# Sparse second feed-forward: a three-stage pair pipeline with six input slots, shared pairs first

## The reference, cut to what matters

```python
logits = x_flat @ gate_w.T                     # 16 experts in 4 groups
scores = sigmoid(logits)
# the best 2 of 4 groups, then the best 4 experts of these; weights renormed, times 2.5
inter = silu(g) * u                            # g, u: 256 -> 128, per expert
expert_out = inter @ down.T                    # 128 -> 256
y = sum over the 4 chosen experts of weight * expert_out
shared_out = silu(x @ shared_gate.T) * (x @ shared_up.T) @ shared_down.T
x = x + tanh(g_ffn[1]) * (y + shared_out)      # with x layer-normed ahead
```

## Time and profile before

| | us |
|---|---|
| median of 2 runs | 1687.89 (1682.67 to 1693.12) |
| the profiled execution's own time | 1683.4 |
| its span, from the first to the last instruction | 1681.6 |
| of it `moe`, from its first weight DMA to the end | 1084.1 to 1681.6 |

### The profile page before, as it was taken

The page is one execution under the profiler, slowest core; times in us unless marked ns, Lnnn a source line. Parts: engine busy times, 40 slices in busy tenths (PEclk is TensorE's granted clock), DMA queues, the critical chain, the costliest instruction groups (busy, mean ns, idle before and its releaser), DMA issues. The chain is left out here.

```text
span 1681.6 us, 27903 instructions
## 1 busy us (share of the span) xinstructions
PE 1214.9 (72%) x9252; PEld 1108.6 (66%) x9252; DVE 950.1 (56%) x2126; ACT 790.8 (47%) x2137; POOL 529.8 (32%) x590
## 2 busy tenths in 40 slices
PE   3675129995899999999999998667773545478772
PEld 2554128884788888888888887567663535367662
DVE  5886845551766666786677777556641212134664
ACT  4554125451566666666565655346442222245441
POOL 4342263642000010003530356163343342444432
PEclk8766559997999999999999999779886676789886
DMA  3354834545000000002420133276233333344785
GB/s 95 135 160 121 180 120 124 147 116 135 7 8 7 8 20 26 8 1 69 133 64 2 64 127 128 64 224 179 86 123 110 92 106 99 96 145 135 251 281 214
DMA packets 135394, 177.12 MB, mean 105 GB/s; under 512 B 17856, under 2 KB 116320, under 8 KB 135264
## 3 DMA queue, kind: packets, MB, share of 16 engines
q1 hardware_dynamic: 107888, 123.67, 25.3%
q0 software_dynamic: 17792, 43.14, 8.0%
q10 hardware_dynamic: 9584, 8.60, 1.6%
HBM read 107.28 MB, written 68.09 MB: 104 GB/s over the span
## 5 line engine op out<-in xcount | busy, mean ns | idle before, releaser
L1587 ACT ACTIVATE attend_s<-attend_s,attend_less 128x128 f32<-128x128 f32 x512 | 198.3, 391 | 107.8 <-DVE attend_less L1728 104.4
L2199 POOL DMA_INDIRECT answers<-moe_yb,moe_dst x160 | 156.4, 978 | 271.9 <-ACT moe_yb L2264 234.5
L2432 PE MATMUL moe_psX<-const_ident,moe_xg 128*128 128x128 f32 x384 | 71.4, 318 | 133.6 <-DMA moe_xg<-slots 126.7
L2313 DVE TENSOR_TENSOR moe_il<-moe_psI,moe_ih 128x256 fp32r<-128x256 f32 x96 | 40.4, 421 | 216.2 <-ACT moe_ih L2248 209.6
L1198 POOL DMA_INDIRECT slots<-router_row,router_idx x128 | 129.4, 1011 | 101.2 <-DMA router_row<-normed_rows 69.6
L1542 POOL TENSOR_TENSOR router_xn<-rest_acc,router_mv 128x512 f32<-128x512 f32 x12 | 12.5, 1045 | 447.5 <-DVE router_rs L1230 391.3
L2432 PEld LDWEIGHTS moe_psX<-const_ident,moe_xg 128*128 128x128 f32 x384 | 52.7, 163 | 137.1 <-DMA moe_xg<-slots 129.6
L81 PE MATMUL moe_psU<-moe_wh,moe_xl 128*128 (+1 forms) x384 | 131.5, 342 | 0.0
L82 PE MATMUL moe_psU<-moe_wl,moe_xh 128*128 (+1 forms) x384 | 120.2, 313 | 0.0
L83 PE MATMUL moe_psU<-moe_wh,moe_xh 128*128 (+1 forms) x384 | 119.5, 311 | 0.0
L81 PE MATMUL moe_psY<-moe_wh,moe_il 128*128 (+1 forms) x192 | 66.1, 344 | 66.8 <-DVE moe_il L2313 60.0
(11 more groups left out here) (367 smaller groups left out, 4209.4 us busy)
## 6 DMA issues: line engine op xcount, KB each, us to landing
moe_xg<-slots SPq DMA_DIRECT2D x160, 129.0 KB
router_row<-normed_rows SPq DMA_DIRECT2D x64, 256.0 KB
moe_big<-answers SPq DMA_DIRECT2D x16, 1024.0 KB
layer_raw<-in_wi_dram SPq DMA_DIRECT2D x8, 1024.0 KB, 5.0
layer_raw<-in_wo_dram SPq DMA_DIRECT2D x8, 1024.0 KB, 7.0
moe_raw<-in_gex_dram SPq DMA_DIRECT2D x17, 384.0 KB
slots<-moe_big SPq DMA_DIRECT2D x32, 129.0 KB
mix_xin<-in_x_dram SPq DMA_DIRECT2D x8, 512.0 KB, 3.8
```

Of the source, the lines that this page charges most:

```text
L1587: last = nc.scalar.activation(s[:, g, j, :], s[:, g, j, :], ACT.Exp, bias=less[:, g, j:j + 1], accum_out=sm[:, g, j:j + 1])
L2199: nc.gpsimd.indirect_dma_start(out=R.YT[q], out_offset=bass.IndirectOffsetOnAxis(ap=dst[:, j % NX, s:s + 1], axis=0), in_=yb[:, j % NY, s, ...
L2313: v.tensor_tensor(il[:], psI[:, 0:N], ih[:], ALU.subtract).then_inc(i_lo, 1)
L2432: last = nc.tensor.transpose(psX[j % 2][:, k * N + s * P:k * N + (s + 1) * P], xg[:, j % NX, s, k * P:(k + 1) * P], C["ident"][:])
```

## The change

Only `moe` and what feeds it change. The numbers of pairs and their order stay: all 16 shared pairs in front (`FIRST, LATE = 16, 0`).

1. Three stages in place of two. PE in turn j does `up(j)`, `turn(j+2)`, `turn_inner(j-1)`, `down(j-2)`; the loops run to 98 turns. `ih`, `il` get two buffers. ACT: `silu(j)`, `x_high(j+2)`, `i_high(j-1)`, `y_out(j-2)`.
2. NX 4 to 6, NY 3 to 5. Weight and target are no longer copied out: ACT and the indirect DMA read them from `xg` in place, the target as an integer. So a routed slot of `xg` is free only when the answers of its pair are written.
3. A shared pair is added by DVE straight from `psY`; POOL and ACT have no part in it.
4. The weights run at two experts a turn: the low half of the odd ones on POOL, between the sends of chunk 3.
5. The rows of the last chunk go through a ring of four (`row`, in the memory of `yt`), the sends begin at turn 22 instead of 27.
6. The padding comes from a DRAM tensor `fill`, written early in the kernel (four more DMAs there, 4.2 MB), DRAM to DRAM.
7. The answers come batch by batch (512 KB), three slots. The routing steps move ahead: 13, 15, 17, 20 in place of 18, 20, 22, 25.

```diff
-            sp.dma_start(rows_[:, :, 0:D], zero.unsqueeze(1).to_broadcast([P, E1, D])).then_inc(self.spare_in, 16)
-            sp.dma_start(rows_[:, :, D:WIDE], self.spare[:, q]).then_inc(self.spare_in, 16)
-        sp.wait_ge(self.spare_in, 64)
+            for kind, to in enumerate((self.fill[q], spare)):
+                rows_ = to.rearrange("(t p) n -> p t n", p=P)
+                sp.dma_start(rows_[:, :, 0:D], zero.unsqueeze(1).to_broadcast([P, E1, D])).then_inc(self.spare_in, 16)
+                sp.dma_start(rows_[:, :, D:WIDE], self.marks[:, q, kind]).then_inc(self.spare_in, 16)
+        sp.wait_ge(self.spare_in, 128)
...
-    NX, NY, NR = 4, 3, 2
-    CB = 2
+    NX, NY, NR, NT, NS = 6, 5, 2, 3, 4
...
-        exps_at, groups_at, experts_at, weights_at, placed_at = 17, 18, 20, 22, 25
+        exps_at, groups_at, experts_at, weights_at, placed_at = 11, 13, 15, 17, 20
...
+        def scattered(eng, r):
+            eng.wait_ge(y_free[r % NY], 32 * (r // NY + 1))
...
             def load(j):
                 b = j % NX
                 if j >= NX:
-                    sp.wait_ge(t_done, j - NX + 1)
+                    if is_shared(j - NX):
+                        sp.wait_ge(t_done, j - NX + 1)
+                    else:
+                        scattered(sp, NTH[j - NX])
...
-                if j - NX >= SHARED_PAIRS:
-                    sp.wait_ge(d_up, j - NX - SHARED_PAIRS + 1)
...
+            for j in range(NX, PAIRS_ALL):
+                i = j - NX
+                for k in (2 * i + NR, 2 * i + NR + 1):
+                    if k < EXPERTS:
+                        weights(k)
+                if j in (7, 9, 11):
+                    R.load_row(sp, LAST - 1, (j - 5) // 2, 0)
+                    R.load_row(sp, LAST - 1, (j - 5) // 2, 1)
+                if j in (8, 10, 12, 14):
+                    R.store_normed(sp, LAST, (j - 8) // 2)
...
+            for t in range(4):
+                R.send(pool, LAST - 1, t)
+                low(4 * t + 1)
+                low(4 * t + 3)
+            for j in ROUTED:
                 scatter(j)
+                i = j - sends_from
+                if i == 0:
+                    pool.wait_ge(R.idx_up, LAST + 1)
+                if 0 <= i < 2 * HALVES:
+                    if i % 2 == 0:
+                        mark(i // 2)
+                    send(i // 2, i % 2)
...
+            def add(j):
+                dve.wait_ge(y_done, j + 1)
+                a = rows(acc[:, 2 * NTH[j]:2 * NTH[j] + 2, :])
+                v.scalar_tensor_tensor(a, psY[j % 2][:], C["gate"][:, 3:4], a, ALU.mult, ALU.add).then_inc(added, 1)
...
+            for j in range(PAIRS_ALL + 2):
...
+                if j < PAIRS_ALL:
+                    up(j, bases[j])
...
                 if j + 2 < PAIRS_ALL:
                     turn(j + 2)
+                if 1 <= j <= PAIRS_ALL:
+                    turn_inner(j - 1)
+                if j >= 2:
+                    down(j - 2, bases.pop(j - 2))
```

More of the change, by code:

```diff
@@ L1087, in __init__ @@
         self.YT = [nc.dram_tensor(f"answers{q}", ((PART_B[q] * TOP + 2 * E1) * P, D), F32, kind="Internal").ap() for q in range(2)]
+        self.fill = [nc.dram_tensor(f"fill{q}", (E1 * P, WIDE), F32, kind="Internal").ap() for q in range(2)]
     def stage(self, m):
-        self.spare = m.sb("spare", [P, 2, E1, 2])
+        self.marks = m.sb("marks", [P, 2, 2, E1, 2])
         self.spare_up, self.spare_in = m.sem("spare_up"), m.sem("spare_in")
@@ L1094, in gpsimd @@
         nc = self.nc
-        nc.gpsimd.memset(self.spare[:], 0.0).then_inc(self.spare_up, 1)
+        nc.gpsimd.memset(self.marks[:], 0.0).then_inc(self.spare_up, 1)
         pool.wait_ge(self.spare_up, 1)
         for q in range(2):
-            last = nc.gpsimd.iota(self.spare[:, q, :, 1], [[P, E1]], base=(PART_B[q] * TOP + E1) * P, channel_multiplier=1, allow_small_or_imprecise_dtypes=True)
+            for kind in range(2):
+                last = nc.gpsimd.iota(self.marks[:, q, kind, :, 1].bitcast(I32), [[P, E1]], base=(PART_B[q] * TOP + E1 * kind) * P, channel_multiplier=1)
         last.then_inc(self.spare_up, 1)
@@ L1116, in __init__ @@
         m = Space(nc, ctx, "router", "right")
-        self.XS, self.YT = kept.XS, kept.YT
+        self.XS, self.YT, self.fill = kept.XS, kept.YT, kept.fill
         self.nc, self.A = nc, A
@@ L2057, in r_bank, with is_shared @@
             return psR
+        def is_shared(j):
+            return KIND[j] == "shared"
         def place_w(k):
@@ L2110, in padded @@
                     sp.wait_ge(table_up, 2 * q + 1)
[L2111 to L2115, removed]
+                first = sp.value_load(tail[0:1, q, e:e + 1], min_val=0, max_val=E1 * REGION[q] - P)
+                sp.dma_start(R.XS[q][bass.ds(first, P), :], R.fill[q][e * P:(e + 1) * P, :]).then_inc(pad_in, 16)
@@ L2134, in answered @@
+                if k >= NT:
+                    store(k - NT)
+                b = k - PART_START[q]
+                sp.dma_start(yt[:, k % NT], R.YT[q][b * P * TOP:(b + 1) * P * TOP, :].rearrange("(p k) d -> p (k d)", k=TOP)).then_inc(yt_in[k % NT], 16)
             def answered(q):
-                last = STARTS_OF[q] + TILES_OF[q] - 1
-                for j in range(last - NY + 1, last + 1):
-                    y_read(sp, j)
+                first = sum(TILES_OF[0:q])
+                for r in range(first + TILES_OF[q] - NY, first + TILES_OF[q]):
+                    scattered(sp, r)
@@ L2145, in _ @@
             R.load_row(sp, LAST - 1, 0, 1)
[L2146 to L2159, removed]
-                if j == STARTS_OF[0]:
[L2161 to L2166, removed]
+            for j in range(1, NX):
+                load(j)
@@ L2167, in _ @@
                 if j == STARTS_OF[1]:
-                    ready(1, LAST + 1)
+                    ready(1)
                 load(j)
-                if j == STARTS_OF[1] + 7:
+                if j == answered_from:
                     answered(0)
[L2172 to L2175, removed]
-                answers(k)
@@ L2177, in _ @@
[L2177 to L2182, removed]
+                for k in asked_at.get(j, []):
+                    answers(k)
+            for j in range(PAIRS_ALL, answered_from + PART_B[0]):
+                for k in asked_at.get(j, []):
+                    answers(k)
+            answered(1)
+            for k in range(PART_B[0], B):
+                answers(k)
@@ L2184, in _ @@
+            for k in range(B - NT, B):
+                store(k)
+            sp.wait_ge(stored, 16 * B)
         @block.gpsimd
@@ L2419, in _ @@
                     combine(k)
-            i_low(PAIRS_ALL - 1)
-            for k in range(COMBINES[0], sum(COMBINES)):
+            for k in range(PART_B[0] + 4, B):
                 combine(k)
```

323 lines of the change are left out of this document (162 added, 161 removed).

## The result

The changed kernel takes 1705.38 us (median of two runs, 1698.44 to 1712.32) against 1687.89: 1.0125 times as long, with a 95% interval of 1.0077 to 1.0173. The forecast was 1701, and a time within 2% of the kernel before. The profiled execution took 1698.44 us, with a span of 1696.7, 15.1 more than before. The two runs of the changed kernel lie 13.9 us apart, so differences of a few us between two traces are to be read with care.

A forecast was written before the change was run, and what follows sets the result against it. Waits bound it, no full engine: in the long stretch PE for `xg`, SP for row sends. Last landing 1674.5 plus 23.0 gives span 1697.5, with 1.8 around it 1699.4, said as 1701 for the median; range 1650 to 1755.

The forecast's parts named there:

- The main term: Routed pairs: an `xg` slot, freed only when its answers are written, closes a loop over two PE turns: 6.1 us a pair.
- T: Pace of the routed pairs, (L + v) / 2: 6.1 us a pair, far ends 5.15 and 7.7.
- L: Loop part from the start of `y_out` through scatters, landing, SP and new load to the next `y_out`: 10.2 us.
- v: Loop part on PE from `turn(j+6)` to the end of `down(j+2)`: 1.4 us at full clock, 2.8 lower, 2.0 taken.
- The front: Stretch before pair 16, bound by splitting weights through two raw slots: pair 16 at 1188 instead of 1180.5, +8 us.
- A round of four experts: In the front: POOL subtractions, weight landing, copy, hand-over, SP, refill and four sends with marks, 17.9 us in sum.
- The routed part: From pair 21 at 1211: 55 turns at 6.1 and 18 at 6.4, 451 us, to 1660; pair 95 at 1664.5.
- The end: Behind pair 95: `down(95)` one turn later, last scatter landed at 1674.5, then 23 us for the answers, as before.
- 1 (T of 5.2 to 5.5): Routed pairs: the loop turns quicker, with loads of 2.1 to 2.5 us; at 5.25 a pair 1639 us; chance 0.15.
- 2 (PE stays cold, T 6.7): Routed pairs: PE never returns to 2.4 GHz, v 2.8, L 10.7, 46 us more: 1747; chance 0.28.
- 4 (slots don't bind): Routed pairs: POOL, PE and 5.0 us a pair set the pace, 290 us instead of 451, about 1540; chance 0.05.
- 3 (a worse front, 1717): Front: refills at 7 us, subtractions of POOL and DVE in each other's way: 1717 us; chance 0.05.

The follow-up runs named there:

- experiment 1: Changed kernel with each row's target and weight copied by DVE out of `xg`, so a slot is free once turned and copied: 1584.53 us, ratio 0.943.
- experiments 1 to 3: Each against the changed kernel: target and weight copied out of the slot, 1584.53 us; seven `xg` slots, answer ring of 4, 1607.86 us; five slots, 2101.72 us.
- experiments 5 and 6: Changed kernel, weight subtractions on DVE, padding behind the weights: 1687.06 us. Kernel of experiment 1 with those subtractions: 1572.34 us; with late padding as well: 1565.87 us.
- experiments 7 and 9: Kernel of experiment 1 with ACT's `x_high` before `silu`: 1591.41 us. Copy, DVE subtractions and late padding together, with four POOL memsets a pair from 58: 1570.33 us.
- experiment 9: Changed kernel with copy, DVE subtractions and late padding (1565.87 us), plus four waited-for POOL memsets behind each pair's scatters from pair 58: 1570.33 us, ratio 0.935.

## Why the prediction came out right, point by point

**What bounds the kernel, and what the change removes.** Right. The wait on sends is gone from the changed kernel. (25.6 us of it come back once the slots no longer bind, experiment 1.)

**The main term.** Right, and shown by experiments 1 to 3: a slot freed at the landing of its answers sets the pace of all routed pairs. T was put at 6.1 us with 6.4 at the end; it is 5.97, 5.67 and 6.26. The two halves, taken for each of the pairs 16 to 89 from the starts of `y_out` and of the first transpose: L is 9.8 us in the mean (10.2 in the prediction) and v 2.2 (2.0). Their sum is twice the pace by the way they are taken, so it is the split that tests the prediction. Inside L each term is within 0.5 us in the mean: from `y_out` to the second scatter 2.4 us (2.87 predicted), its landing 3.0 in the 44 rounds in which SP's wait for it can be seen (2.7), SP 0.84 and the second load 0.71 (0.92 and 0.60), from there to the turn 2.84 (3.1 and 0.04). In the bare loop with five slots the same terms are 2.4, 2.4, 0.8, 0.6 and 2.2 us, and L is 8.5: with six slots the loop is 1.3 us longer, nearly all of it in the landings. The prediction said that SP's refills, padding and answers, and POOL's sends, run beside the loop at no cost. But it took its landings from rows of a crowded round, which may have held that cost already. Which neighbour takes how much was not measured.

The 6.4 us at the end came out (6.26), but not for the reason given. It was put to DVE, which waits in `combine`. PE waits 4.4 us for DVE in that stretch and 35.7 us for `xg`, and the landing of the answers is 3.6 us in the mean of the pairs 74 to 89 where it is 2.7 in the pairs 57 to 73: the loop is longer.

Of the signs, SP's waits are 3.5 us each without the first, as said, but 42 and not 70 of them, and PE's idle time before the turn is 1.9 us a pair, in 48 waits, and not 3.

The Trainium skill, "DMA: Bandwidth & Descriptors", section "Anatomy of one DMA", gives 2.0 us and bytes over 436 GB/s, for DMAs that GpSimd issues. By it a 128 KB transfer takes 2.3 us, an estimate. The scatter's 2.41 in the bare loop agrees; the load, issued by SP, takes 2.06 there. With six slots both take longer, 3.0 and, up to the turn, 2.84. With 2.3 for both and the v of 2.0 that the prediction chose the pace is 5.5, with the full-clock v of 1.4 it is the 5.2 of the prediction; both are too short.

**The front.** The step that was mis-sized. Turn 8 was put at 1160 and pair 16 at 1188; they are at 1170.5 and 1199.3. A round of four experts was put at 17.9 us. The POOL subtractions that begin the rounds start at 1098.2, 1115.9, 1137.0 and 1158.3: 17.6, then 21.2 and 21.3. What the 3.3 more a round are is in POOL's timeline of the changed kernel, one row of the second round and one of the third:

```profile
1125.52 1.83 POOL L2229 TENSOR_TENSOR moe_wl<-moe_raw,moe_wh 128x768 fp32r<-128x768 f32 x1 [7.86 <-ACT moe_wh L2280]
...
1152.58 1.01 POOL L1202 DMA_INDIRECT slots<-router_row,router_idx  x1 [6.88 <-DMA router_row<-normed_rows]
```

From the end of the first subtraction of a round to the end of the second it was 5.8 us in the sum (landing of the weights 2.9, copy, hand-over, subtraction); it is 5.9, then 9.7, then 6.6. In the second round the weights take 4.0 us to land (issued 1117.7, landed 1121.7), and ACT copies them only at 1124.6, behind a `silu` for which it had to wait. From there to the first send it was 4.6 (0.9 and 3.7); it is 4.7, 4.5 and 7.1. The sends and the next subtraction are as predicted or shorter. So the terms that were too small are the landing of weights and rows and ACT's wait between them; this makes 5.3 of the 10.5 us. The rest lies behind the last of these subtractions, 12.1 us to turn 8 where 7 was put, and was not taken apart. And the padding was "costed at nothing", because SP was idle in the stages looked at; in the front SP isn't idle, and experiments 5 and 6 give the padding a price of 5.4 to 7.7 us there. The eight turns from there to pair 16 took 28.8 us, 28 was predicted.

**From pair 16 to 21** it was put at 23 us and is 20.5. So pair 21 is 9 us late, not 11.

**The routed part** was put at 453.5 us from pair 21 to 95 and is 441.1: 12.4 less, from the pace. **The end** was put at 33.0 us behind pair 95 and is 35.8. In all 9 more, 12 less and 3 more: the span was put at 1697.5 and is 1696.7. The main term was right within 3%; that the span is right within 1 us is luck, since the miss in the front and the miss in the pace cancel.

**The rivals.** 1 (T of 5.2 to 5.5): seen in places, three successive rounds near 1420 to 1441 us take 9.9 to 10.3 us for two pairs, but not in the mean. 2 (PE stays cold, T 6.7): v is over 2.8, the value of the lower level, in 25 of 74 rounds and under 2.0 in 34. PE had waited more than 2 us just before 23 of the 25 and before 7 of the 34, so it does fall back in these gaps; the stretches have a clock of 0.79 to 0.82. That part of the rival is seen in a third of the rounds, but L is 9.8 and not the 10.7 that it needed. 4 (slots don't bind) was what the change seems to promise, and experiment 1 is that kernel: 1584.5, where 1540 was said. 3 (a worse front, 1717) was right in kind: turn 8 came 10.5 us later than forecast.

## What to carry to other kernels

Count a ring's slots from the event that frees them, not from their number: in the stretches without sends a pair took 5.7 us with six slots freed at the landing of the results and 4.1 us with four freed at the first read. A write, its landing, a wait on the queue and a new load lie in the loop (8 to 10 us here); divide that by the turns it spans before calling a ring deep. If small fields keep a large buffer alive, copy them out: a copy of 0.16 us was worth 7% of the changed kernel. And a queue that is idle in one stage may be the bound of another; cost the writes that are moved there stage by stage.

## What the runs showed of the hardware that was not expected

A DMA costs SP more than its issue where its address is read first. The issue of a load of `xg` takes 0.33 us and that of a padding write mostly 0.51. But each padding write has its own `value_load` and address arithmetic, and four in a row take 4.45 to 4.95 us, 1.1 to 1.2 each.

PE's signals to other engines can come 1 us to several us after the work that they stand for, several at once, and the engine that waits for them starts 0.02 us after the signal (300 of 311 late starts in the twelve traces; for the other 11 no signal is on record near the start). This is not bound to the slot freed early: there are 12 such starts from pair 22 on in the kernel before, 14 in the changed one, 44 with the copy (experiment 1) and none with five slots. 303 of the 311 fall in a run of four or more indirect DMAs that POOL issues without a break (experiments 7 and 9). The cause stays open; a version in which POOL's scatters are spread without added work was not tried. In experiment 9, with memsets between them, the pairs of the dense end came 0.15 to 0.2 us faster each.
